# A four-layer decoder on one core: loads at other times, the third layer's experts in tiles of 128 rows, the last cross attention in one block

## What is computed

```python
x = _layernorm(x + _L0_ffn_ref(x, ...))                 # 8 experts of 512 hidden, top 2, behind an attention
x = _layernorm(x + _L1_ffn_ref(x, ...))                 # 8 experts of 1024 hidden, one chosen by a floor of a key
x = _layernorm(x + _L2_ffn_ref(x, ...))                 # 8 experts of 256 hidden, top 2, and a shared one
x = _layernorm(x + _L3_xattn_ref(x, ctx_1024, ctx_1024))
x = _layernorm(x + _L3_ffn_ref(x, ...))
```

```python
kv_mat = jnp.einsum('bsd,bse->bde', k * scale, v)       # 256 x 256, k = v = ctx
out = jnp.einsum('bsd,bde->bse', q * scale, kv_mat)
```

## Time and profile before

| | us |
|---|---|
| runs, without a profile | 2792.64, 2781.83, 2787.05; median 2787.05 |
| profiled execution | 2783.7 |
| its span, first to last instruction | 2781.4 |

### The profile page before, as it was taken

The page is one execution under the profiler, slowest core; times in us unless marked ns, Lnnn a source line. Parts: engine busy times, 40 slices in busy tenths (PEclk is TensorE's granted clock), DMA queues, the critical chain, the costliest instruction groups (busy, mean ns, idle before and its releaser), DMA issues. The chain is left out here.

```text
span 2781.4 us, 38610 instructions
## 1 busy us (share of the span) xinstructions
PE 2228.1 (80%) x14546; PEld 1479.6 (53%) x14591; DVE 1534.8 (55%) x3069; ACT 931.8 (33%) x1526; POOL 815.4 (29%) x602
## 2 busy tenths in 40 slices
PE   6978839883895881995778777969999997768998
PEld 5765535552794771994446634853434433354554
DVE  3774773456234565113724541336998999735553
ACT  3423313321112241332233310126757564413331
POOL 1121321224002102002220113034887988502221
PEclk9989969996897885997999988989999999979999
DMA  4217010001993102992000004742111020010000
GB/s 153 70 39 239 13 61 2 1 17 46 356 383 118 39 8 108 372 351 97 8 24 1 2 12 148 202 147 84 31 31 43 19 58 4 0 50 1 8 9 16
DMA packets 104439, 234.30 MB, mean 84 GB/s; under 512 B 9984, under 2 KB 77312, under 8 KB 95296
## 3 DMA queue, kind: packets, MB, share of 16 engines
q1 hardware_dynamic: 96576, 210.86, 21.8%
q0 software_dynamic: 7680, 20.98, 2.4%
HBM read 175.83 MB, written 55.97 MB: 83 GB/s over the span
## 5 line engine op out<-in xcount | busy, mean ns | idle before, releaser
L3557 POOL TENSOR_TENSOR l_attn_ring<-l_attn_ring,l_attn_c_rows 128x1024 f32<-128x1024 f32 x128 | 302.1, 2360 | 85.9 <-DVE l_attn_ring L3446 85.9
L3446 DVE TENSOR_TENSOR_SCAN l_attn_ring<-bank,l_attn_ring 128x512 f32<-128x512 f32 x256 | 299.1, 1210 | 23.2 <-ACT bank L3332 18.7
L163 PE MATMUL bank<-x_features,weights 128*128 128x512 f32 x544 | 259.9, 623 | 25.9 <-ACT x_features L3296 8.4
L3176 PE MATMUL bank<-l_attn_ring,identity 128*128 128x512 f32 x512 | 251.1, 613 | 35.8 <-POOL l_attn_ring L3557 28.9
L3332 ACT ACTIVATE bank<-l_attn_step,l_attn_minus_exp_a_log 128x508 f32<-128x508 f32 x256 | 173.6, 685 | 162.3 <-DVE l_attn_ring L3446 161.9
L163 PEld LDWEIGHTS bank<-x_features,weights 128*128 128x128 f32 x544 | 106.1, 199 | 152.9 <-issue 129.5
L3176 PEld LDWEIGHTS bank<-l_attn_ring,identity 128*128 128x128 f32 x512 | 95.8, 194 | 150.5 <-issue 104.1
L457 DVE TENSOR_REDUCE negmax_slots<-bank 128x16 f32<-128x2048 f32 x48 | 109.8, 2288 | 102.3 <-PE bank L349 102.0
L3752 PE MATMUL bank<-l_ffn_hidden_parts,l_ffn_sign_weights 128*128 128x512 bf16 x752 | 165.1, 379 | 0.8
L3440 DVE TENSOR_TENSOR l_attn_ring<-l_attn_step_times_input,bank 128x1024 f32<-128x1024 f32 x128 | 153.4, 1199 | 3.4 <-PE bank L3162 1.6
L3752 PEld LDWEIGHTS bank<-l_ffn_hidden_parts,l_ffn_sign_weights 128*128 128x128 bf16 x768 | 75.2, 98 | 90.0
(11 more groups left out here) (652 smaller groups left out, 4468.9 us busy)
## 6 DMA issues: line engine op xcount, KB each, us to landing
l_attn_tile_weights<-l_ffn_experts SPq DMA_DIRECT2D x23, 2180.0 KB, 9.8
ffn_experts_tile_weights<-l_ffn_experts_experts SPq DMA_DIRECT2D x39, 1024.0 KB, 7.8
expert_slots<-zeros SPq DMA_DIRECT2D x8, 2048.0 KB, 13.1
l_attn_c_rows<-state_outputs SPq DMA_DIRECT2D x64, 256.0 KB, 3.3
l_ffn_tile_weights<-l_ffn_experts SPq DMA_DIRECT2D x23, 512.0 KB, 4.6
expert_slots<-residual_sum SPq DMA_DIRECT2D x62, 128.0 KB, 8.4
expert_slots<-zeros SPq DMA_DIRECT2D x1, 5888.0 KB, 28.5
l_ffn_tile_x<-expert_slots SPq DMA_DIRECT2D x23, 256.0 KB, 4.4
```

What stands on the lines that cost most here:

```text
L163: mm = pe.matmul(out, w[:, f, m * P:(m + 1) * P], src[:, f, :], start=start and f == 0, stop=stop and f == k - 1)
L3176: mm = pe.matmul(net.banks[SUMS[j]][:], net.ident[:], ring[n % 4][:, j, :], start=s == 0, stop=s == STATES - 1)
L3446: nc.vector.tensor_tensor_scan(ring[n % 4][:, j, :], net.banks[DECAY[j]][:], ring[n % 4][:, j, :], 0.0, ALU.mult, ALU.add).then_inc(state_ ...
L3557: tt(ring[n % 4][:], ring[n % 4][:], c_row[:, n % STATES, :].unsqueeze(1).broadcast_to([P, 2, T]), ALU.mult).then_inc(out_ready, 1)
```

## The change

Five places.

1. `start`: SyncE issues the identity, x, the weights, then (each behind the transposes that free its room) contexts 2 and 3, then the other 12 constants. ScalarE issues contexts 0 and 1 at once. TensorE waits for the identity, and for each group of x on its own.
2. First layer's experts: the weights of tiles 0 and 1 are loaded at the end of the stage before, into `xT_all`, as soon as the table is there (`load_first_weights`); the six rooms then hold tiles 2 to 7. The stores of x stand in fours behind tiles 5, 8, 11 and 14, `prefetch` behind tile 18, `load_groups` behind tile 24.
3. Second layer's experts: tile 0's weights are loaded at the end of the stage before, likewise; `prefetch` stands behind tile 8.
4. Third layer's experts: tiles of 128 rows, 39 of them, with the same 4 rooms, now also 4 for rows and 4 for results. ScalarE stores tile t-1's result behind tile t's activation. `prefetch` comes first in the stage.
5. `l3_xattn` is one block over all groups: TensorE does the context products of group g+1 ahead of the outputs of group g, four context buffers instead of two, the norms of groups 0 to 2 on GpSimd (`Norms.normalise`, L276 to L279), of group 3 on VectorE, the root on ScalarE.

```diff
-TILE_ROWS = {"l0_ffn_experts": 128, "l1_ffn": 128, "l2_ffn": 256}
+TILE_ROWS = {"l0_ffn_experts": 128, "l1_ffn": 128, "l2_ffn": 128}
...
             def _(sp):
                 prefetch(sp)
+                sp.wait_ge(table_ready, 1)
+                load_first_weights(sp, net, "l0_ffn_experts")
...
+def first_weights(net, name):
+
+    room = net.xT_all[:].rearrange("p g f t -> p (g f t)")
+    if name == "l0_ffn_experts":
+        return [(room[:, 2048 * t:2048 * (t + 1)], None) for t in range(2)], 32
+    if name == "l1_ffn":
+        return [(room[:, 0:4096], net.ctx_room[0][:].rearrange("p b d -> p (b d)")[:, 0:8 + D])], 64
+    return [], 0
+
+
+def load_first_weights(sp, net, name):
+    params, table, cols = net.params[name + "_experts"], net.routing.table, EXPERT_COLS[name]
+    for t, (both, biases) in enumerate(first_weights(net, name)[0]):
+        n = both.shape[1]
+        at = sp.value_load(table[0:1, 1, t:t + 1], min_val=0, max_val=(EXPERTS - 1) * cols)
+        sp.dma_start(both, params[:, bass.ds(at, n)]).then_inc(net.first_weights, 16)
+        if biases is not None:
+            sp.dma_start(biases, params[:, n:][:, bass.ds(at, cols - n)]).then_inc(net.first_weights, 16)
...
+    def room_of(self, t):
+        return (t - len(self.first)) % self.rooms
...
         def load_w(t):
-            if t >= self.rooms:
+            if t < len(self.first):
+                return
+            if t >= len(self.first) + self.rooms:
                 sp.wait_ge(self.out_in_psum, t - self.rooms + 1)
...
-        prefetch(sp)
         for t in range(self.tiles):
             if t + early < self.tiles:
                 load_x(t + early)
                 load_w(t + early)
-            sp.wait_ge(self.out_ready, t + 1)
-            sp.dma_start(self.tile_rows(row[t]), self.y[t % self.y_rooms] if self.blocks == 1 else self.y[t % self.y_rooms][:]).then_inc(
-                self.stored[t % self.y_rooms], 16)
+            if not self.stored_by_act:
+                self.store(sp, t, row[t])
             if t in at_tile:
                 at_tile[t](sp)
...
+    def store(self, engine, t, row):
+        engine.wait_ge(self.out_ready, t + 1)
+        y = self.y[t % self.y_rooms]
+        engine.dma_start(self.tile_rows(row), y if self.blocks == 1 else y[:]).then_inc(
+            self.stored[t % self.y_rooms], 16)
...
                 ins.then_inc(self.hidden_ready, 1)
+            if self.stored_by_act and t:
+                self.store(act, t - 1, self.row_of(act, t - 1))
+        if self.stored_by_act:
+            self.store(act, self.tiles - 1, self.row_of(act, self.tiles - 1))
...
-        def store(sp):
-            for g in range(GROUPS):
-                net.store_across(sp, g)
+        beside = {5 + 3 * g: lambda sp, g=g: net.store_across(sp, g) for g in range(GROUPS)}
+        beside[18], beside[24] = prefetch, net.load_groups
...
-                experts.run_sp(sp, prefetch, {0: store, 8: net.load_groups})
+                experts.run_sp(sp, beside)
...
-                experts.run_sp(sp, prefetch)
+                experts.run_sp(sp, {8: prefetch})
...
+                prefetch(sp)
                 sp.wait_ge(table_ready, 1)
-                experts.run_sp(sp, prefetch)
+                experts.run_sp(sp)
```

The new `l3_xattn`, its TensorE part and the end of its VectorE part:

```diff
+                products(0)
+                for g in range(GROUPS):
+                    if g + 1 < GROUPS:
+                        products(g + 1)
+                    outputs(g)
+                    if g >= 2:
+                        turn(g - 2)
+                turn(GROUPS - 2)
+                turn(GROUPS - 1)
...
+                    if g >= 2:
+                        take(g - 2)
+                dve.wait_ge(x_ready, last)
+                for n in range(last, SEQUENCES):
+                    norms.normalise(nc.vector, dve.wait_ge, n, x_all[:, n, :], x_all[:, n, :], x_ready)
+                take(GROUPS - 2)
+                take(GROUPS - 1)
+
+            @block.gpsimd
+            def _(pool):
+                for n in range(last):
+                    norms.normalise(nc.gpsimd, pool.wait_ge, n, x_all[:, n, :], x_all[:, n, :], x_ready)
```

and the start:

```diff
                 def _(sp):
+                    sp.dma_start(net.ident[:], consts["ident"]).then_inc(ident_ready, 16)
                     for g in range(GROUPS):
-                        sp.dma_start(net.x_all[:, g * NB:(g + 1) * NB, :], x_g[g]).then_inc(io_done, 16)
+                        sp.dma_start(net.x_all[:, g * NB:(g + 1) * NB, :], x_g[g]).then_inc(x_landed[g], 16)
                     load_weights(sp, SUBLAYERS[0])
+                    for g in range(2, GROUPS):
+                        sp.wait_ge(ctxT_in_psum, 2 * g - 2)
+                        sp.dma_start(net.ctx_room[g % 2][:], ctx_g[g]).then_inc(net.ctx_ready[g % 2], 16)
...
                 def _(act):
+                    for g in range(2):
+                        act.dma_start(net.ctx_room[g][:], ctx_g[g]).then_inc(net.ctx_ready[g], 16)
```

181 lines of the change are left out of this document (129 added, 52 removed).

## The result

The changed kernel takes 2758.0 us (median of four runs, 2756.6 to 2763.2) against 2784.4 (2780.0 to 2792.6) for the one before: a ratio of 0.9905, with a 95% interval of 0.9877 to 0.9933, 26.4 us faster. The forecast was 2741, 46 us faster, in a range that ends at 2759. So the direction and the range held, and 20 us of the gain are missing.

A forecast was written before the change was run, and what follows sets the result against it. TensorE is busy 80% of the span, so the other 20% can go, sought stage by stage. The five stages' terms, -5 - 10.5 - 3.7 - 1.8 - 25, sum to -46 us: 2741 us, range 2725 to 2759.

The forecast's parts named there:

- Forecast as it stands: Whole kernel: the summed gains of all five stages hold, 2741 us, own range 2733 to 2750; chance 0.48.
- rival A: Third layer: the rooms rule, a tile takes 2.6 us, 12 us more than forecast, 2753 in all; chance 0.17.
- so I price it at nothing: First layer: two tiles' weights loaded during the stage before cost 0, as POOL's scattering ends that stage.
- at most the 2.5 us a 1 MB load takes: First layer: upper cost of the early weights if they lost the cover of POOL's scattering.
- the 2.0: First layer's start: x loads go first in the queue and land earlier, gaining 2.0 us.
- the removed wait: First layer: TensorE's 6.9 us wait for an x tile, behind SyncE's 16 x stores, goes.
- a third wait: First layer: another wait for x tiles, behind the group loads, goes with its restart, 1.4 us.
- beneath POOL's scattering: Second layer: one tile's weights come early, hidden under the scattering that ends the stage before, at no cost.
- limit (b): Third layer: a room's turn bounds a tile at (0.75 + L + 0.1 + 1.95) / 3, 2.23 us, L being the weights' landing.
- so I take 3.9: Third layer: weights land 3.9 us after issue, below the earlier least of 4.2, since x and y tiles are halved.
- SyncE's 2.2 us: Third layer: SyncE's two loads a tile at 1.11 us each bound the tile at 2.2 us.
- TensorE's 1.95: Third layer: TensorE's own work per tile of 128 rows, 1.95 us, half that of 256 rows.

The follow-up runs named there:

- scalar_x_loads: Changed kernel with six rooms instead of four in the third layer's experts and x tiles loaded by ScalarE instead of SyncE: 2733.9 us, ratio 0.9828.
- tiles_256: Changed kernel with the third layer's experts back in tiles of 256 rows, stored by SyncE: 2745.8 us, ratio 0.9864.

## Why the prediction was right, and where it was off

**The total: right by its range, and narrowly.** 2758.0 is 1 us inside the end at 2759. It is outside the 2733 to 2750 of "Forecast as it stands", for which 0.48 stood, and the range reached it because it took in rival A at 2753. That it held is luck as well: the last cross attention gave 2.8 us more than forecast, 1.5 of it by a clock that rose earlier than its rows had shown, and the kernel before came out at 2784.4 instead of the 2787.05 from which the 2741 was counted. Either of them missing would have put the time beyond 2759.

**Start: right.** -4.3 for -5. Context 2 was expected near 18 and TensorE had it at 19.2.

**First layer: right in kind, but forecast a third too large, by the other kernels nearly twice.** Forecast -10.5, measured -7.5 between last scatter and next stage in the changed kernel, and -4.6 to -6.6 in the table's variants. Two terms were off. The step "so I price it at nothing" for the early weights failed, and its own fallback ("at most the 2.5 us a 1 MB load takes") was near the value: with 2 MB of weights under way the scatters' last rows land 2.0 us later and the stage starts 1.9 us later, which leaves 0.3 of the 2.0. And the removed wait was counted with 1.5 us of restart and 1.4 of a third wait; from first transpose on, 7.2 came for 8.5 (4.7 to 6.1 in the variants), with one wait of 1.41 still there. A piece of four stores was priced at 4.1 us and took 2.5 to 2.7 in the changed kernel. The step also saw only the 16 stores as cause and passed over the 770 KB that moved with them; with the stores in fours each of the other two edits could be taken back alone without the wait coming back.

**Second layer: the mechanism right, the size wrong.** The first transpose comes 3.9 us sooner behind the scatter, and the wait for the second tile's weights is 1.70 as written. But 3.0 us of the stage's start were priced at nothing, "beneath POOL's scattering". Taken into the sum they leave -0.7 of the -3.7; measured were -0.1 in the profiled execution of the changed kernel and -0.8 to -1.3 in the others.

**Third layer: the wrong step.** This is where the gain went: +11.4 for -1.8, 13 of the 20 us that are missing. The limits were the right ones, and limit (b), the room's turn, rules; what failed is "so I take 3.9" for the landing L, argued from x and y tiles of half the size. It started from the least value of the earlier trace rows, 4.2, and went below it; the median there is 4.6, and with that the same formula already gives 2.47. Measured is 4.9: the transfers come one and a half times as often, and the traffic rose from 270 to about 300 GB/s. Over all kernels the landing goes with the traffic: 4.3 and 4.6 us at about 270 GB/s, 4.9 at 275 to 304, 5.1 at 321 to 334, 5.8 and 6.3 at 365 to 403. Put into the same formula, (0.75 + 4.9 + 0.1 + 1.95) / 3 = 2.57; measured 2.61. That is rival A with its 2.6, for which 0.17 stood. The estimate of 3.2 by the Trainium skill (DMA: Bandwidth & Descriptors, Anatomy of one DMA) is off by more in the same direction; the section gives its fit for DMAs that GpSimd issues, these are SyncE's, and their medians of 4.3 to 6.3 us do not agree with it. The rest of the price list held: SyncE's 2.2 us is what six rooms ran into (2.29), TensorE's 1.95 is what scalar_x_loads reached (2.00), ScalarE's store costs nothing visible and its issue takes 0.34 to 0.40 us.

**Last cross attention: right, 2.8 us low.** -27.8 for -25; the stage takes 40.5 us where the prediction's own times make 42.9. The products of the first two groups took 8.67 us together instead of 10.2, because the granted clock rises 3 us into them, where the earlier trace rows had the first 6.69 mostly at the low one; all behind that is earlier by these 1.5. Of the rest, one term is a copy that stands with 1.4 us in the sum to 2481.7 and takes 0.7; what remains is open. Windows of the changed kernel:

```profile
2446.80:2449.80 3.00, 3.00 (x7) 2.47 (x8) 0.00 (x0) 0.75 (x2) 0.00 (x0) 0.50 0.57 159
2449.80:2452.80 3.00, 3.00 (x15) 2.59 (x15) 0.00 (x0) 1.79 (x3) 0.00 (x0) 0.99 1.16 392
```

**The sum.** Stage by stage, for the first and second layer with the middle of the runs that share the stage: -4.3, -6.0, -1.1, +11.4, -27.8, together -27.8; the medians say -26.4. The stages add up as supposed. The profiled execution alone shows 20.0, 6 us less than the medians. Its own five stages make -28.3, and 8.9 us came back in two stretches whose work is the same: 4.4 between the start and the last scatter ahead of the first layer's experts (660.5 before, 664.9 here, 656 to 665 in the other kernels), and 4.5 from the first layer's end to the last scatter of the second, which took 233.4 us in the changed kernel, 227.9 in tiles_256, 221.3 to 234.3 in the others and 228.9 before. Windows of 40 us from about 115 us into that stretch, changed kernel, then tiles_256:

```profile
970.00:1010.00 40.00, 37.58 (x227) 32.39 (x229) 21.81 (x73) 17.43 (x30) 0.00 (x0) 0.79 0.04 14
```

```profile
965.00:1005.00 40.00, 34.60 (x261) 28.72 (x263) 25.46 (x79) 21.63 (x36) 0.00 (x0) 0.96 0.04 14
```

The granted clock is 0.79 in the one and 0.96 in the other, with 227 and 261 matmul instructions in the window. What lowers it at one time and not at another stays open.

**Slips in the prediction's sums** that change nothing: with 2.6 us a tile its own steps for the third layer make about +10.2 and not +10.6, and bytes of 1.9 us in 2.25 are 84% and not 88%.

## What to carry to other kernels

Smaller tiles halve the work that hides a load but not its latency: with weights of fixed size per tile, take the time per tile as no less than (release to issue + landing + use) / (rooms - 1), with a landing of the traffic that the change itself makes and never below the median of the rows, and give rooms and issuing engines before cutting the tile; 128-row tiles lost 11 us with four rooms and won 12 over the old ones with six and x on another queue. Transfers moved "beneath" another engine's work have to be priced against the landing of that work's own last transfer, not against the engine. Where several edits relieve the same wait, test them two by two: each of them can look like the whole cause or like nothing.

## What was not expected of the hardware

- A DMA share of 0.92 was no full queue: at 287 to 304 GB/s the stage waited for landings, and the same transfers ran at 400 GB/s (share 1.05) with six rooms and x from another engine's queue.
- 2.0 and 2.2 MB of weights from SyncE, issued while GpSimd's indirect scatters ran, left the scatters' own times on GpSimd alone (0.96 us each, 1.26 apart), let their rows land 2.0 and 3.6 us later behind the last of them, and moved the start of the next stage by 1.9 and 3.0 us.
- 16 stores of 128 KB hold SyncE for 12.1, 14.5, 15.0 or 16.4 us, by what else is in the queue; in fours they cost 2.5 to 2.7 in the changed kernel, 0.65 each, and the first four up to 3.7 in others.
